# Both boundaries of a sorted expert layer: weights of two blocks split beforehand, first supertile combined tile by tile, unread products in TensorE's stops

## The reference

```
x = x + attention(layernorm(x))            # 64 sequences of 64 tokens, 8 heads, latent keys and values
x = x + experts1(layernorm(x), ctx)        # top 2 of 8 experts by ctx @ Wg + bg; relu MLP 128 -> 512 -> 128
x = x + experts2(layernorm(x))             # top 8 of 32 experts in 4 of 8 groups; silu-gated MLP 128 -> 64 -> 128, and a shared one
```

## Time and profile before

| | us |
|---|---|
| median of 3 runs | 734.87 (734.66 to 737.75) |
| profiled execution, its own time | 733.23 |
| its span, first to last instruction | 731.5 |
| TensorE busy in the span | 651.3 (89%) |
| VectorE busy | 546.1 (75%) |
| ScalarE busy | 352.0 (48%) |
| GpSimd busy | 339.5 (46%) |
| mean granted TensorE clock | 0.958 |

### The profile page before, as it was taken

One profiled execution on the slowest core, in us unless ns is written; L12 is line 12 of the kernel. 1 busy time (PEld: TensorE's weight loads), 2 busy tenths in 40 slices (PEclk: granted clock), 3 DMA queues, 4 the chain that ended last, 5 costly groups with the idle time before them and its releaser, 6 DMA issues. The chain is left out here.

```text
span 731.5 us, 10866 instructions
## 1 busy us (share of the span) xinstructions
PE 651.3 (89%) x3356; PEld 457.1 (62%) x3356; DVE 546.1 (75%) x1321; ACT 352.0 (48%) x636; POOL 339.5 (46%) x383
## 2 busy tenths in 40 slices
PE   6878788786779999999982998999999999999997
PEld 6545455554657777777761665666666666666664
DVE  4478888879248999999964695877778695958564
ACT  3846677653026666666663434344343435253221
POOL 5112588777858999999956423050503122000000
PEclk9968999989889999999995999999999999999999
DMA  8910400000124566676211474463544645354442
GB/s 220 360 43 0 110 30 30 34 26 37 48 88 125 167 180 202 180 195 179 79 57 45 92 173 117 113 144 108 141 108 124 145 120 137 90 140 111 127 116 58
DMA packets 74967, 84.13 MB, mean 115 GB/s; under 512 B 15441, under 2 KB 44091, under 8 KB 74910
## 3 DMA queue, kind: packets, MB, share of 16 engines
q1 hardware_dynamic: 69688, 74.93, 37.1%
q0 software_dynamic: 4096, 8.40, 4.0%
q10 hardware_dynamic: 1126, 0.11, 0.1%
HBM read 64.48 MB, written 18.87 MB: 114 GB/s over the span
## 5 line engine op out<-in xcount | busy, mean ns | idle before, releaser
L872 ACT ACTIVATE r_s<-bank 128x512 f32<-128x512 f32 x136 | 81.2, 597 | 150.0 <-PE bank L1442 138.4
L1662 PE MATMUL pair_banks<-t_s,Dn 128*128 128x512 f32 x272 | 138.6, 595 | 1.5 <-issue 1.5
L1182 DVE TENSOR_TENSOR h1l<-r,h1h 128x512 fp32r<-128x512 f32 x92 | 113.0, 1246 | 17.8 <-POOL h1h L588 17.8
L1297 DVE TENSOR_TENSOR rc_s<-r_s,score_banks 128x512 f32<-128x512 f32 x90 | 61.5, 683 | 45.3 <-ACT r_s L872 32.7
L1440 PE MATMUL bank<-fxh,Gh 128*128 128x512 f32 x136 | 95.0, 698 | 0.0
L1310 DVE TENSOR_TENSOR t_s<-rc_s,bcb 128x512 f32<-128x512 f32 x128 | 87.4, 685 | 4.8 <-DMA bcb<-c_rows 4.1
L588 POOL TENSOR_SCALAR h1h<-r 128x512 fp32r<-128x512 f32 x92 | 74.7, 817 | 20.1 <-ACT r L818 18.0
L607 POOL TENSOR_TENSOR mvp<-mvp,meps 128x4 f32<-128x4 f32 x8 | 1.6, 199 | 169.9 <-DVE mvp L1220 168.5
L546 POOL DMA_INDIRECT x_sorted<-xsb,posi x64 | 64.4, 1006 | 29.6 <-DVE xsb L1098 16.4
L599 POOL DMA_INDIRECT yg<-y_sorted,posi x64 | 62.9, 983 | 24.9 <-issue 18.4
L1662 PEld LDWEIGHTS pair_banks<-t_s,Dn 128*128 128x128 f32 x272 | 51.5, 190 | 16.5 <-issue 5.8
(11 more groups left out here) (290 smaller groups left out, 1572.4 us busy)
## 6 DMA issues: line engine op xcount, KB each, us to landing
bcb<-c_rows SPq DMA_DIRECT2D x128, 256.0 KB
wraw<-in_L_xattn_W SPq DMA_DIRECT2D x46, 256.0 KB, 2.8
x_sorted<-wraw SPq DMA_DIRECT2D x1, 5888.0 KB, 17.4
xg<-x_sorted SPq DMA_DIRECT2D x23, 256.0 KB, 3.6
y_sorted<-ysb SPq DMA_DIRECT2D x23, 256.0 KB, 3.1
ctxb<-in_ctx SPq DMA_DIRECT2D x8, 256.0 KB, 6.1
out<-x_all SPq DMA_DIRECT2D x8, 256.0 KB
x_all<-in_x SPq DMA_DIRECT2D x2, 512.0 KB, 5.2
```

The costliest lines, as they stand in the source:

```text
L872: act.activation(r_s[:, n % RB2, :], bank[n % 3][:, :], ACT.Silu).then_inc(F["act"], 1)
L1182: tt(h1l[:, n % NB1, :], r1[:, n % RB1, :], h1h[:, n % NB1, :].bitcast(F32), ALU.subtract)\
L1297: tt(rc_s[:, n % CB2, :], r_s[:, n % RB2, :], bank[3 + n % 3][:, :], ALU.mult).then_inc(F["rc"], 1)
L1662: mm(bank[6][:, :], Dn[:, weights_of(p), :], t_s[:, n % TB2, :], start=(p == 0), stop=(p == NC2 - 1))\
```

## The change

1. **Sorted layer, first two blocks.** POOL does `w_high` of both matrices of blocks 0 and 1 and `w2_low(0)` ahead of the loop, DVE `w1_low(0)` and `w1_low(1)`. The loop does these steps only for later blocks (`w2_low(1)` stays).
2. **Unread products, sorted layer.** PE does 14 products identity by identity (128x128 by 128 columns, `unread`) into bank 2 after `to_features(0)`, and 12 more ahead of the first product of block 1.
3. **First supertile of the routed layer.** A semaphore for each tile in place of each half; DVE combines tile by tile, with statistics and aggregate in the same turn (`combine_first`). DVE normalises tiles 0 and 1 (`normalise_first`) while ACT does tiles 2 and 3. PE turns the rows twice, into bank 5 and bank 7; DVE copies `xTt` from bank 5 (`features_first`) while ACT copies `fxh` from bank 7. The logits go to bank 4 and no longer wait for `fxl`; product 1's up half waits for the scores.
4. **Unread products, routed layer.** PE does 16, 16, 16 and 8 as the four tiles arrive, then 8 each after the last statistics, the aggregate, the first `rstd` step and `nb`: 88 in all, ahead of `prep_x(0)`.
5. **Lag.** `weighted` runs 9 products behind at first (`START`), and comes down by one every 3 products to 5; `CB2` goes from 10 to 13.
6. Semaphores merged at the attention's start and for `out_bias`.

```diff
-LAG2, RB2, CB2, TB2 = 3, 4, 10, 6
-BEHIND, EARLY = 5, 5
+LAG2, RB2, CB2, TB2 = 3, 4, 13, 6
+BEHIND, START, EARLY = 5, 9, 5
@@ weighted_at
-        last = max(1, done, n + 1 - min(BEHIND, left))
+        behind = max(BEHIND, min(START, START - (n - START) // 3))
+        last = max(1, done, n + 1 - min(behind, left))
@@ POOL, sorted layer
             w_high(0, 0)
+            w_high(1, 0)
+            w_high(0, 1)
+            w2_low(0)
+            w_high(1, 1)
             for n in range(NCB):
                 b, c = n // FB, n % FB
-                if c == 0:
+                if c == 0 and b >= 2:
                     w_high(b, 1)
-                if c == 1 and b + 1 < NBK:
+                if c == 1 and 2 <= b + 1 < NBK:
                     w_high(b + 1, 0)
-                if c == 2:
+                if c == 2 and b >= 1:
                     w2_low(b)
@@ DVE, sorted layer
             w1_low(0)
+            w1_low(1)
             sorted_low(0)
@@
-                if c == 1 and b + 1 < NBK:
+                if c == 1 and 2 <= b + 1 < NBK:
                     w1_low(b + 1)
@@ PE, sorted layer
             to_features(0)
+            unread(bank[2], 14)
             for n in range(NCB + LAG1 + 3):
+                if n == FB:
+                    unread(bank[2], 12)
@@ PE
+            def unread(where, count):
+                for _ in range(count):
+                    mm(where[:, 0:P], ident[:, :], ident[:, :], start=True, stop=True)
@@ ACT
-                for t in range(TPS):
+                for t in range(2 if j == 0 else 0, TPS):
                     ins = act.activation(xnp[:, t, :], x_all[:, j * TPS + t, :], ACT.Identity, bias=nb[:, t, :],
@@ DVE, routed layer
-            combine(0, 0)
-            combine(0, 1)
-            aggregate(0)
+            def combine_first(t):
+                dve.wait_ge(s_yg0[t], 32)
+                for c in range(2):
+                    if c == 1:
+                        dve.wait_ge(F["cmb1"], t + 1)
+                    xr = x_all[:, t, :]
+                    dve.scalar_tensor_tensor(xr, yg[:, 0, t, c, :], wts[:, t, c:c + 1], xr, ALU.mult, ALU.add)\
+                        .then_inc(F[("cmb1", "cmb")[c]], 1)
+                dve.wait_ge(F["cmb"], t + 1)
+                dve.bn_stats(st6p[:, t, :], x_all[:, t, :]).then_inc(F["bst"], 1)
+                dve.wait_ge(F["bst"], t + 1)
+                ins = dve.bn_aggr(mvp[:, t, :], st6p[:, t, :])
+                if t == TPS - 1:
+                    ins.then_inc(F["pstat"], 1)
+
+            def normalise_first():
+                for t in range(2):
+                    ins = ts(xnp[:, t, :], x_all[:, t, :], mvp[:, t, 0:1], mvp[:, t, 1:2], ALU.subtract, ALU.mult)
+                ins.then_inc(F["pxv"], 1)
+
+            def features_first():
+                dve.wait_ge(F["pxT_ps"], 1)
+                dve.tensor_copy(xTt[:, :], bank[5][:, :]).then_inc(F["xT"], 1)
+
+            for t in range(TPS):
+                combine_first(t)
             negated_mean(0)
+            normalise_first()
+            features_first()
             low_x(0)
@@ PE, routed layer
+                if n == 1:
+                    pe.wait_ge(F["sc"], 1)
@@ PE, prep_x
+                if j == 0:
+                    pe.wait_ge(F["pxv"], 1)
+                    for t in range(TPS):
+                        transpose(bank[5][:, t * P:(t + 1) * P], xnp[:, t, :])
@@ PE, prep_logits
-                pe.wait_ge(F["fxl"], j + 1)
+                if j >= 1:
+                    pe.wait_ge(F["fxl"], j + 1)
@@ PE
+            pe.wait_ge(s_f2l, NG)
+            for t in range(TPS):
+                pe.wait_ge(s_yg0[t], 32)
+                unread(bank[6], 16 if t < TPS - 1 else 8)
+            for ready in (F["bst"], F["pstat"], F["prstd"], F["pnb"]):
+                pe.wait_ge(ready, TPS if ready is F["bst"] else 1)
+                unread(bank[6], 8)
             prep_x(0)
             prep_logits(0)
-            pe.wait_ge(s_f2l, NG)
             prep_back(0)
```

More of the change, by code:

```diff
@@ L288, in gate_bank1, with logit_bank @@
             return bank[(0, 1, 4, 5)[n % 4]]
+        def logit_bank(j):
+            return bank[4 if j == 0 else 7]
         def sem(name):
@@ L305, in decoder_kernel @@
         s_yg = [[sem(f"gathered{i}_{h}") for h in range(2)] for i in range(2)]
+        s_yg0 = [sem(f"gathered_first{t}") for t in range(TPS)]
         s_pchain, s_dchain = sem("pool_chain"), sem("dve_chain")
@@ L314, in decoder_kernel @@
         s_rows, s_rowsS = sem("rows_spread"), sem("rows_read")
-        s_hps, s_hq, s_hk, s_hv = (sem(n) for n in ("heads_transposed", "hq", "hk", "hv"))
-        s_gps, s_G, s_ops, s_N = (sem(n) for n in ("absorbed", "absorbed_read", "out_absorbed", "out_absorbed_read"))
+        s_hps, s_hqk, s_hv = (sem(n) for n in ("heads_transposed", "hq_and_hk", "hv"))
+        s_gps, s_G, s_ops, s_N = (sem(n) for n in ("absorbed", "absorbed_read", "out_products", "out_products_read"))
         s_gsplit, s_gb, s_orow, s_cnt = sem("attn_weights_split"), sem("keys_low"), sem("orow"), sem("counts_read")
@@ L325, in decoder_kernel @@
             "up gate act rc t dn accS tp x2 cmb1 cmb bst pstat prstd pnb pxn pxT_ps fxh xT fxl lg lgS back sc cw c_ps cT "
-            "chain").split()}
+            "chain pxv").split()}
         s_cs = sem("c_rows_out")
@@ L596, in gather @@
                 if j >= 2 and t == 0:
-                    pool.wait_ge(F["cmb"], 2 * (j - 1))
+                    pool.wait_ge(F["cmb"], TPS + 2 * (j - 2))
                 for c in range(2):
@@ L601, in gather @@
                         in_offset=bass.IndirectOffsetOnAxis(ap=posi[:, j * TPS + t, c:c + 1], axis=0))\
-                        .then_inc(s_yg[j % 2][t // 2], 16)
+                        .then_inc(s_yg0[t] if j == 0 else s_yg[j % 2][t // 2], 16)
             def rstd(j):
@@ L646, in _ @@
             act.wait_ge(s_consts, 1)
-            copy(hq[:, :, 0:QR], heads[0]).then_inc(s_hq, 1)
+            copy(hq[:, :, 0:QR], heads[0]).then_inc(s_hqk, 1)
             act.wait_ge(s_hps, 3)
@@ L682, in out_bias @@
             def out_bias():
-                act.wait_ge(s_obb, 1)
-                copy(obb[:, :], bank[7][:, 3 * D:4 * D]).then_inc(s_obbS, 1)
+                act.wait_ge(s_ops, 2)
+                copy(obb[:, :], bank[7][:, 3 * D:4 * D]).then_inc(s_N, 1)
             def normalise1(m, t):
@@ L833, in prep_x @@
                 copy(fxh[:, (j % 2) * ST:(j % 2 + 1) * ST], bank[7][:, :]).then_inc(F["fxh"], 1)
-                copy(xTt[:, :], bank[7][:, :]).then_inc(F["xT"], 1)
+                if j >= 1:
+                    copy(xTt[:, :], bank[7][:, :]).then_inc(F["xT"], 1)
             def prep_lg(j):
                 act.wait_ge(F["lg"], j + 1)
-                copy(lgS[:, :], bank[7][:, 0:P]).then_inc(F["lgS"], 1)
+                copy(lgS[:, :], logit_bank(j)[:, 0:P]).then_inc(F["lgS"], 1)
             def prep_sc(j):
                 act.wait_ge(F["back"], j + 1)
-                act.activation(scores[:, :, :], bank[7][:, P:P + TPS * E2].rearrange("p (t e) -> p t e", t=TPS),
+                act.activation(scores[:, :, :], logit_bank(j)[:, P:P + TPS * E2].rearrange("p (t e) -> p t e", t=TPS),
                                ACT.Sigmoid).then_inc(F["sc"], 1)
@@ L1070, in add_out_bias @@
                 if m == 0:
-                    dve.wait_ge(s_obbS, 1)
+                    dve.wait_ge(s_N, 2)
                 dve.wait_ge(A["xn"], m + 1)
@@ L1200, in combine @@
             def combine(j, h):
-                dve.wait_ge(s_yg[j % 2][h], 64 * (j // 2 + 1))
+                dve.wait_ge(s_yg[j % 2][h], 64 * ((j + 1) // 2))
                 for c in range(2):
                     if c == 1:
-                        dve.wait_ge(F["cmb1"], 2 * j + h + 1)
+                        dve.wait_ge(F["cmb1"], TPS + 2 * (j - 1) + h + 1)
                     for t in (2 * h, 2 * h + 1):
@@ L1209, in combine @@
                     ins.then_inc(F[("cmb1", "cmb")[c]], 1)
-                dve.wait_ge(F["cmb"], 2 * j + h + 1)
+                dve.wait_ge(F["cmb"], TPS + 2 * (j - 1) + h + 1)
                 for t in (2 * h, 2 * h + 1):
@@ L1215, in aggregate @@
             def aggregate(j):
-                dve.wait_ge(F["bst"], 2 * (j + 1))
-                if j >= 1:
-                    dve.wait_ge(F["pxn"], j)
+                dve.wait_ge(F["bst"], TPS + 2 * j)
+                dve.wait_ge(F["pxn"], j)
                 for t in range(TPS):
@@ L1354, in _ @@
                 ins.then_inc(s_hps, 1)
-            pe.wait_ge(s_hq, 1)
-            pe.wait_ge(s_hk, 1)
+            pe.wait_ge(s_hqk, 2)
             for h in range(H):
@@ L1428, in out_bias @@
                 pe.wait_ge(s_orow, 1)
-                mm(bank[7][:, 3 * D:4 * D], onesM[:, :], obz[:, :], start=True, stop=True).then_inc(s_obb, 1)
+                mm(bank[7][:, 3 * D:4 * D], onesM[:, :], obz[:, :], start=True, stop=True).then_inc(s_ops, 1)
             def ranks():
@@ L1518, in values @@
                 if n == 0:
```

(8 more changed lines are left out.)

3 lines of the change are left out of this document (1 added, 2 removed).

## The result

The changed kernel took 758.74 us (median; 752.4 to 759.89), the kernel before, beside it on the same chip, 736.2: ratio 1.029, 95% interval 1.025 to 1.033. It is slower by 2.9% where 1% faster was forecast. A second comparison on another chip gave 1.022 (1.016 to 1.028), with 753.3 us. The profiled execution took 759.63 us, its span is 757.9 against 731.5, so 26.4 us are to be found.

A forecast was written before the change was run, and what follows sets the result against it. TensorE was taken as nearest to full, so time won at a boundary reaches the end whole. Boundary terms 4.2 + 3.2 = 7.4 us, from 734.87 to 727.5 us; range 722.5 to 731.7.

The forecast's parts named there:

- The price of an unread product: Both boundaries: 0.114 us each; the first 14 take 1.6 us without delay, the second fill delays the transposes by 1.0.
- the fill at the wrong clock: Rival, both boundaries: clock already fallen, each unread product takes 0.114 more, 2.5 and 1.6 us; 731.6 us, chance 0.08.
- Boundary 1, forecast 4.2: Sorted layer's start: block 1 starts 2.6 us sooner, block 2 4.2 sooner, all kept to the end; bounds 2.6 and 5.0.
- the chain of the forecast: Inside block 1, without POOL's `W2h(1)`: steps from `r(5)` at 217.45 to `xl(2)` at 220.7 start block 2 at 220.8.
- Boundary 2, first product 2.4 sooner: Routed layer's start: first product at 397.1 at full clock, 2.4 us sooner; whole boundary 3.2 us, bounds 1.0 and 8.5.
- the rival of a blocked gather: Second boundary: `normalise_first` blocks issue of tile 5's gathers, everything up to `cw` 2 to 2.5 us later; 729.7, chance 0.08.
- The lag, `cw` 5.0 sooner less 2.6 owed: Routed layer, supertile 1: `cw` 5.0 us sooner, TensorE still owes three `down_product`, 2.6 us; net 2.4.
- `fxl`, 0.8 us won: Routed layer: the later TensorE wait of 0.75 us for `fxl(2)` goes because DVE is there first, 0.8 won.
- Late gathers: Rival, slower: supertile 2's gathers among 16 `bcb` transfers arrive after DVE wants them, up to 6 us delay; chance 0.04.

The follow-up runs named there:

- rearrangement: Kernel before plus the second boundary's combining by tiles, four more transposes and logits in the other bank; old weight split and lag, no unread products: 730.4 us, 0.997.
- ring-of-13 kernel: Changed kernel without unread products, with the old lag (START = 5) but the longer ring (CB2 = 13): 727.3 us, 0.992 of the kernel before.
- the fill that fits: Changed kernel with old lag, no sorted-layer unread products, nine 512-column ones at the second boundary: 727.3 us against 733.1 for the kernel before, 0.992.

## Why the prediction was wrong

**The price of an unread product, the step that failed.** "36 of this kind took 4.29 us, 0.114 each". The row counts records, and a float32 product leaves two; 36 records are 18 products, 0.23 us each. The profile before had shown it: `down_product` runs 8 x 17 = 136 times and stands with x272, and the text ahead of the prediction itself calls it shown as two matmuls. The 14 were charged 1.6 us and take 3.3, so the first product is late by 1.6 (charged: nothing). At the second boundary I let the fill start at 384.25 and the last eight end at 394.4, some 10.2 us. With 88 at 0.224 they take 19.7 us at best, from 389.10 to 408.8: 10 us past the end of the last tile's scaling (397.56 + 0.89), not 1.0. They took 27.6, from 389.10 to 416.7: 4.7 of the other 7.9 us are the six stops, and about half of what is left, by an estimate from the granted clock of 0.94 over these 27 us, is the half clock behind them. So of the 17.4 us by which the fill outlasted its forecast the halved price is some 9.5, an estimate from these rows, and the stops with what follows them are the rest, for which the sum had no term.

**Fill and clock.** The rival "the fill at the wrong clock" was the only one that asked what the fill may cost, and it asked for 0.114 more on each. The true price was that much more, at the full clock; and that a stream of 128-column products can stand still on its own was not among the rivals at all.

**Boundary 1, forecast 4.2.** The split with half the fill or none gives 3.4 us in six profiles (11.8 us for the first two blocks, against 15.3) and 2.6 to 2.8 in two. Block 1 starts 4.9 us after block 0, 2.6 us sooner as forecast; it then lasts 6.93 us, where the chain of the forecast had 6.2. So the mechanism held, and 0.9 us came from inside block 1 in place of 1.6. The clock was at 1.00 from 205 to 225 in all six, four of them without any fill there, and fell to 0.78 and 0.67 in the two slower: it goes with 0.7 to 0.9 us, and is mostly full without a fill. With 12 products ahead of it, block 1 starts after 5.9 us; with the 14 as well, 0.9 us is left of the 3.4.

**Boundary 2, first product 2.4 sooner.** Without fill it is 2.0 us sooner (19.2 to 19.4 after the first gather, 21.33 before), so tile-wise addition, the two banks and the split of the scaling between VectorE and ScalarE hold together; none of the three was timed alone. The rearrangement as a whole measures 0.997. The gather behind `rstd` took 1.01 us beside `normalise_first`, and also 1.01 in the kernel before, with nothing of VectorE beside it: the rival of a blocked gather is out. The 3100 ns that the Trainium skill gives for such a DMA beside a DVE copy (SBUF — State Buffer, "A bandwidth-pool intuition that's wrong (but worth ruling out)") are not seen here.

**The lag, `cw` 5.0 sooner less 2.6 owed.** This failed by itself, and apart from the fill. `cw` did not come nearer to the first product (41.3 us before; 42.7 with the change, 42.8 with the lag alone; single profiles with the short lag have 40.4 to 43.2). I counted what VectorE no longer does, and missed two new stops of TensorE: 3.2 to 4.0 us for the logits' turn, in six of the seven profiles with the longer lag and in none of the others, and 2.1 to 2.4 us for `fxl` later, in all seven. Each brings a stretch of half clock (0.62, 0.58). One profile with the short lag has a stop for `fxl` too, 2.9 us at another supertile. I had promised the reverse for `fxl`, 0.8 us won. From the turn of `cw` to the end the changed kernel takes 5.2 us more; 2.6 of it are what the sum had put down as owed, an estimate from its own term, and the 2.3 us stop for `fxl` is nearly the rest. Why the first stop comes is open: ScalarE's own stop ("remote", for which the profile names no source) is 3.3 us in the kernel before too, at 424, and TensorE works through it there; the DMA share is 1.05 to 1.09 in the ring-of-13 kernel too, which has no such stop at all.

**Late gathers** as the way to be slower: not seen in the changed kernel, where VectorE waits for no `yg` between 396 and 470. In the kernels with the short lag it does wait, for 1.6 us with the fill that fits and 1.4 with the ring of 13, and those two are the fastest measured: the wait that the prediction feared is real and small.

Without its fill and lag the change gives 5.2 us in the medians (733.1 to 727.9, interval 2.9 to 7.0) where the sum had 7.4.

## What to carry to other kernels

Before a row's time is divided by its count, the count is to be checked against the program: a loop whose number of products is known tells how many records one leaves. A filler on the critical queue must be shown to end before the work behind it can start, with its price doubled as a test; if it must exist, few wide products did it better here than many small ones, and even a fill that cost nothing won nothing, since VectorE set the next step. And a new lag between dependent products is an edit of its own: it should be timed alone, for its gain on paper is only what one engine no longer does.

## What the runs showed of the hardware

- Products of 128 columns ran at one record per 0.112 to 0.115 us for 42 to 45 records, then TensorE stood six times within some 12 us, up to 1.74 us, and later ran 87 or 93 records on end. At the first boundary 28 and 24 records ran without a stop. Wide ones of the same columns never stood (10.35 us for 22 records).
- ScalarE stood 3.3 to 5.4 us on "remote" while transfers filled the DMA engines (share 1.06), in four of the seven profiles with the longer lag and, for 3.3 us, in two of the seven with the short one. VectorE stood for 2.3 to 3.1 us on "remote" in three of those with the longer lag. What they waited for no row names.
- The half clock early in the attention falls at other places from one execution to the next (0.50 to 0.54 in 44 to 60 us before; 0.50 to 0.55 in 52 to 64 and 76 to 88 after), and the last scatter lies between 200.9 and 208.4 us, latest (207.3 to 208.4) in the five profiles that have both of the later stretches. With single profiles, absolute times can't be compared across kernels; distances from a common instruction can.
